# A state-space scan with a routed feed-forward part: one softplus, two row Silus, one block of drives and the last output products change places

## The reference, cut to what matters

```python
xn = layernorm(x)                                     # 2 rows of 1024 tokens, 512 wide
proj = xn @ W_in.T; x, gate = halves of 1024
x = silu(causal conv of x with 4 taps)
ts, Bm, Cm = rms(parts of x @ W_x.T)                  # 32, 16, 16 wide
dt = softplus(ts @ W_dt.T + b_dt)
state = state * exp(dt * A) + (dt * x) * Bm           # scan over time, 1024 channels x 16 states
y = (sum over states of state * Cm + x * D) * silu(gate)
s = y @ W_out.T
g = silu(top-2-of-8 experts of xn)                    # each token: weighted sum of two expert rows
out = x_in + s * g
```

## Time and profile before

| | |
|---|---|
| median of three runs | 1031.8 us |
| profiled execution | 1033.03 us |
| its span, first to last instruction | 1031.2 us |
| mean granted TensorE clock | 0.917 |
| busy: DVE, POOL, PE, ACT | 977.1, 908.9, 841.1, 731.3 us |

### The profile page before, as it was taken

How to read it: one execution, slowest core, us unless ns; L and a number is a source line. 1 busy time by engine, 2 the same in 40 slices (tenths; PEclk the granted TensorE clock), 3 DMA queues, 4 the chain that set the end, 5 groups by cost and what they waited for, 6 DMA issues and landing times.

```text
span 1031.2 us, 10504 instructions
## 1 busy us (share of the span) xinstructions
PE 841.1 (82%) x2832; PEld 321.6 (31%) x2832; DVE 977.1 (95%) x1026; ACT 731.3 (71%) x1283; POOL 908.9 (88%) x321
## 2 busy tenths in 40 slices
PE   9953579899788998999647859999887989979477
PEld 6520123333333333333212213333332333323122
DVE  6989999999999989999989899999999999999986
ACT  3657677798787767888655566888778776777542
POOL 0546899999989989998798999899988999999996
PEclk9976679999989999999876889999999999999788
DMA  9875688666777756566733742956648565663735
GB/s 342 333 251 211 227 288 298 258 259 235 266 277 265 263 221 235 210 218 211 235 105 116 234 176 102 321 194 219 208 162 294 171 233 190 224 242 125 272 55 143
DMA packets 82059, 229.22 MB, mean 222 GB/s; under 512 B 8784, under 2 KB 10320, under 8 KB 75344
## 3 DMA queue, kind: packets, MB, share of 16 engines
q1 hardware_dynamic: 67792, 197.08, 53.4%
q0 software_dynamic: 6144, 16.78, 6.3%
q10 hardware_dynamic: 8064, 14.68, 3.8%
HBM read 116.05 MB, written 45.35 MB: 157 GB/s over the span
## 4 chain that ended last, share of the span: by engine, by line
DVE 30%; POOL 22%; PE 17%; issue 14%; ACT 14%; DMA 2%; ACTq 0%; SPq 0%; DVEq 0%; POOLq 0%
POOL drive L622 13%; DVE sc_ps L1221 10%; DVE drive L1221 6%; POOL drive L635 5%; DVE drive L1232 5%; ACT sc_ps L837 5%; PE x_ps L1554 3%; PE dt_ps L1482 3%; PE y_ps L1522 2%; DVE x_ps L1145 2%; PE f_ps L1507 2%; POOL moe L607 2%; ACT L979 1%; PE x_ps L1416 1%; DVE xy L1145 1%
## 5 line engine op out<-in xcount | busy, mean ns | idle before, releaser
L622 POOL TENSOR_TENSOR drive<-rep,b_all 128x2048 f32<-128x2048 f32 x127 | 580.2, 4607 | 21.6 <-DMA rep<-dtu 13.2
L837 ACT ACTIVATE sc_ps<-rep,a_neg 128x512 f32<-128x512 f32 x512 | 332.5, 682 | 96.8 <-DVE drive L1232 73.3
L635 POOL TENSOR_TENSOR drive<-drive,c_all 128x1024 f32<-128x1024 f32 x94 | 225.5, 2399 | 20.4 <-ACT state L816 14.8
L1522 PE MATMUL y_ps<-drive,stack 128*32 128x512 f32 x1024 | 151.5, 666 | 96.6 <-DVE drive L1232 56.5
L1221 DVE TENSOR_TENSOR_SCAN sc_ps<-sc_ps,state,drive 128x512 f32<-128x512 f32 x162 | 200.4, 1275 | 6.4 <-ACT sc_ps L837 2.7
L1232 DVE TENSOR_TENSOR drive<-sc_ps,c_all 128x1024 f32<-128x1024 f32 x161 | 196.0, 1218 | 2.9
L1221 DVE TENSOR_TENSOR_SCAN sc_ps<-sc_ps,drive 128x512 f32<-128x512 f32 x160 | 188.9, 1216 | 7.0 <-ACT sc_ps L837 4.2
L1507 PE MATMUL f_ps<-w_ring,xT_slot 128*128 128x512 f32 x368 | 169.3, 603 | 24.2 <-ACT xT_slot L847 24.2
L1482 PE MATMUL dt_ps<-xnT,w_g 128*128 128x512 f32 x232 | 117.6, 653 | 20.0 <-ACT dtu L804 16.8
L1221 DVE TENSOR_TENSOR_SCAN drive<-sc_ps,state,drive 128x512 f32<-128x512 f32 x94 | 116.3, 1270 | 2.7 <-ACT sc_ps L837 2.6
L1221 DVE TENSOR_TENSOR_SCAN drive<-sc_ps,drive 128x512 f32<-128x512 f32 x96 | 114.6, 1212 | 1.2 <-ACT sc_ps L837 0.6
(11 more groups left out here) (192 smaller groups left out, 1038.2 us busy)
## 6 DMA issues: line engine op xcount, KB each, us to landing
rep<-dtu SPq DMA_DIRECT2D x128, 512.0 KB
w_ring<-wring SPq DMA_DIRECT2D x46, 1024.0 KB, 4.9
x_slot<-slot_x SPq DMA_DIRECT2D x46, 256.0 KB, 4.5
slot_rows<-y_slot ACTq DMA_DIRECT2D x46, 256.0 KB
w_g<-wg_in SPq DMA_DIRECT2D x32, 256.0 KB
w_x<-wx_in SPq DMA_DIRECT2D x24, 256.0 KB
slot_x<-zeros SPq DMA_DIRECT2D x1, 5888.0 KB, 20.3
slot_x<-zeros SPq DMA_DIRECT2D x5, 1024.0 KB, 8.7
```

Of the source, the lines that this page charges most:

```text
L622: pool.tensor_tensor(drive[:, m % RING, :, :], rep[:, n % 2, :, 1, :], b_all[:, q:q + 1, :].broadcast_to([P, NR, TC]), ALU.mult).then_inc( ...
L635: pool.tensor_tensor(drive[:, m % RING, 0:2, :], drive[:, m % RING, 0:2, :], c_all[:, q:q + 1, :].broadcast_to([P, 2, TC]), ALU.mult).then ...
L837: act.activation(sc[:, r, :], rep[:, n % 2, r, 0, :], ACT.Exp, scale=a_neg[:, lo:lo + 1]).then_inc(decay_ok, 1)
L1522: last = pe.matmul(y_ps[CH * r:CH * (r + 1), :], stack[:, :], drive[:, m % RING, r, :], start=False, stop=(m % NQ == NQ - 1))
```

## The change

- In tile 15, DVE's `step_sizes(16)` stands behind the high product of quad 0 instead of ahead of it.
- In tile 16, POOL issues `drives` of quad 3 ahead of `gather_first(1)`, and `drives` of tile 17's quad 0 ahead of `add_second(1)`; before, each stood behind. In tile 30 the order stays.
- In tiles 17 and 31, ACT's `silu_moe` stands between the skip diagonal and the decays of quad 1, between two table loads of its own. Before it shared the block of the gate's Silu. In tile 31 the gate's block moves ahead of the first half decays of quad 2 (`SILU_SOON`). Tile 15 keeps its rows' Silu where it was.
- In tile 31, PE does five of the nine output products that stood behind the sums of quad 1 ahead of them (the four others stay behind); output tile 3 does five instead of six products ahead of the last sums and one behind them, and its last two come after the last products of tiles 0 to 2.

```diff
-SILU_SOON = (24, 25, 26, 27, 28, 29, 30)
+SILU_SOON = (24, 25, 26, 27, 28, 29, 30, 31)
+STEPS_BEHIND = (15,)
+ROWS_FIRST = (17, 31)
...
                 low_products(NQ * n)
-                if gathers:
+                if gathers and not even:
                     gather_first(c - 1)
                 put_rows(*PUTS.get((n, 0), (0, 0)))
                 drives(NQ * n + 3)
                 low_products(NQ * n + 1)
-                if gathers:
+                if gathers and even:
+                    gather_first(c - 1)
+                elif gathers:
                     add_second(c - 1)
...
                 drives(NQ * n + 4)
+                if gathers and even:
+                    add_second(c - 1)
...
                 store_slot(b, left_slot)
+                if n in ROWS_FIRST:
+                    act.preload_act_table_set(SILU)
+                    silu_moe(c - 1, 0, TT)
+                    act.preload_act_table_set(LNEXP)
                 decays(m + 1, 0)
...
                     silu_gate(n)
-                    if (c and even and t == 1) or (not even and t == NT - 1):
+                    if n == PER_ROW * NT - 1:
                         silu_moe(c - 1, 0, TT)
...
-                    if chunk_end and not pe_log(n + 1):
+                    if chunk_end and not pe_log(n + 1) and n not in STEPS_BEHIND:
                         step_sizes(n + 1)
                     if n not in GATE_BEHIND:
                         gate_tile(n - 1)
                     products(m, 1)
+                    if n in STEPS_BEHIND:
+                        step_sizes(n + 1)
...
                 sums(m)
+                if c == NCH - 1 and t == NT - 1:
+                    out_tile(c, 0, t - 1, t)
+                    out_tile(c, 2, t - 1, t)
+                    out_tile(c, 1, 0, 3)
...
                 if c == NCH - 1 and t == NT - 1:
-                    out_tile(c, 0, t - 1, t)
-                    out_tile(c, 2, t - 1, t)
-                    out_tile(c, 1, 0, t)
+                    out_tile(c, 1, 3, t)
                 sums(m + 2)
...
-            out_tile(NCH - 1, 3, 0, NT - 2)
+            out_tile(NCH - 1, 3, 0, 5)
             sums(QUADS - 1)
-            out_tile(NCH - 1, 3, NT - 2, NT - 1)
-            for i in range(TT):
+            out_tile(NCH - 1, 3, 5, 6)
+            for i in range(TT - 1):
                 out_tile(NCH - 1, i, NT - 1, NT)
+            out_tile(NCH - 1, 3, 6, NT)
```

## The result

The changed kernel takes 1034.58 us (median of 20 runs, 1032.96 to 1036.43) against 1032.28 us of the kernel before in 20 runs. The ratio is 1.002, 95% interval 1.0013 to 1.0026: slower by 2.3 us, where 1031.6 and no measurable change were forecast and the range ended at 1034.0. The profiled execution took 1035.1 us with a span of 1033.3 us, 2.1 us longer than the one before.

What follows compares the result with a forecast made beforehand. DVE was taken to bound the kernel, busy 377.6 of 388 us from 612 to 1000 us. Tiles 15 to 17 at +3.0 us and the tail at -3.2 gave -0.2, so 1031.6 us, range 1028.0 to 1034.0.

Steps and rivals of the forecast that it cites:

- Steps 1 and 2: Tiles 15 and 16: softplus behind the high product, drives ahead of gathers; tile 17 begins 3.9 us sooner, last gather 4.6 later.
- step 1: Tile 15, DVE: the 1.21 us product fits into the wait for ACT's logarithm; what is queued behind starts 1.1 us sooner.
- Step 3: Tile 17, ACT: rows' Silu waits for the last gather; quad 1 starts 4.15 us after its landing, break-even landing at 594.3.
- Step 4: Tile 18's spread delays the last gather 3.3 us, to 597.3; tiles 15 to 17 cost +3.0 us (bounds -0.3, +4.9).
- rival B: Spread served first or in equal turns: all 5.2 us added to the gathers, landing 599.2, kernel 1033.5 us; chance 0.17.
- Rival A: Accumulating gathers not held up by the spread: landing 594.0, kernel 1028.3 us; chance 0.23.
- rival D: Another wait in tile 15 or 16 takes the 1.1 us; spread comes later, gather delay 2.6 us, kernel 1030.9; chance 0.12.
- Step 5: Tile 31, ACT: rows' Silu hidden with 1.0 us to spare; DVE's 1.14 us wait in quad 2 goes, gain 1.1.
- Step 6: Tail of tile 31: output products moved into PE's idle time; gain 3.2 us with the ACT edits' gain (bounds -3.4, -2.4).
- sign that the prediction named for being right: Tile 17: Silu about 597, DVE idle some 8 us, no quad 2 wait, step sizes near 586; tile 31: gate about 1 us behind.
- signs for being wrong: Tile 17's rows' Silu by 594 or after 599; tile 31: DVE waiting for quad 1 or 2 decays, or PE's products delaying sums.
- C: Tail of tile 31: TensorE's clock falls in shorter idle times, gain 2.4 instead of 3.2, kernel 1032.4 us; chance 0.08.

Runs made afterwards that it cites:

- Experiment 6: Kernel before with the tile 31 edits and the softplus of step_sizes(16) behind the high product, no other edits: 1030.81 us, ratio 0.9987.
- Experiments 1 and 2: Changed kernel with, first, tile 17's rows' Silu back in the gate's block: 1028.67 us, 0.9964; second, tile 16's gathers ahead of the drives again: 1029.51 us, 0.9974.
- Experiment 3: Changed kernel with SP holding tile 18's spread until tile 16's four accumulated gathers have landed: 1030.15 us, ratio 0.9976.
- experiment 4: Kernel before with the tile 31 edits on ACT and PE alone: 1030.96 us, ratio 0.9985.
- experiment 7: Kernel before with POOL's changed order in tile 16 and no other edit: 1030.66 us, ratio 0.9983.
- experiment 5: Tile 31 edits alone, with POOL's last three residual adds of chunk 2 cut to 8 of 512 columns: 1029.60 us against the kernel before, ratio 0.997.

## Why the prediction was wrong

**Steps 1 and 2 were right.** With the execution's lead of 1.3 us, tile 17 was forecast to begin at 586.0 - 1.3 = 584.7 and begins at 584.78; the last gather is issued at 586.96, forecast at 588.4 - 1.3 = 587.1. Experiment 6 shows that step 1 is worth nothing as long as POOL's drives set the pace of tile 16.

**Step 3 was right in mechanism and sum.** The Silu waits, quad 1 starts 600.83 - 596.61 = 4.22 us behind its start (4.15 forecast), and the whole stands and falls with the landing. Experiments 1 and 2 take away the early Silu and the late gathers, one at a time, and either frees the kernel. Experiment 3 takes away the spread beside the gathers and frees it in part.

**Step 4 had a term too small.** The delay is 4.1 us, not 3.3: 0.9 us for each of the 4.7 us of engine time left, where plain gathers had shown 0.7. That lies between the forecast and rival B, which put all 5.2 us on it. In the profile tiles 15 to 17 cost 3.6 us instead of 3.0. By the ratios of the changed kernel and experiment 4 they cost 0.35%, also 3.6 us, but with some 1.2 us of noise either way, so that the times alone wouldn't tell 3.6 from 3.0. Rival A, no delay, is refuted by the 9.5 us and by experiment 3. What rival D said of the size holds: experiment 7, where the spread comes 0.9 us later against the last gather, has 0.9 us less of delay.

**Step 5 was right.** In tile 31 the rows' Silu is hidden and DVE's wait of 1.14 us is gone.

**Step 6 is the one that failed.** "3.2" was right up to the gate product: 3.4 us of gain there against 3.3 forecast. It was worth 1.5 us in time (ratio 0.9985). I had looked at POOL's last residual adds only for the order of the stores ("its store is queued ahead of the last four") and taken DVE's chain behind the gate product as fixed in length (it is 7.1 us before, 9.3 in the changed kernel). But the gain brings DVE's first add, which reads both operands from SBUF, 3.4 us forward, while POOL's adds don't come sooner (they come 0.6 us later): into POOL's row of adds, which until then had ended 1.6 us ahead of it. It took 2.27 us more, shown with its cause by experiment 5. The Trainium skill, GPSIMD Engine Reference, section Key points, has the rule: GpSimd shares its SBUF interfaces with VectorE, and instructions of VectorE with two SBUF inputs contend. The rows agree: 2.95 us for the add from SBUF, 0.69 us for the products from PSUM beside the same adds.

With tiles 15 to 17 at the profile's 3.6 us and the tail at experiment 4's -1.5 the sum is +2.1 us; 2.3 were measured. Of the 2.3 us between this sum and the forecast of -0.2, 0.6 are step 4's and 1.7 step 6's. Step 6 alone lies outside its noise: experiment 4's interval ends at a gain of 2.6 us, and 3.2 were forecast.

Every sign that the prediction named for being right came true: the rows' Silu at 596.6, DVE idle 8.6 us ahead of quad 1, the gate product 1.27 us behind DVE's last product. None of the signs for being wrong did. They all concern waits, and the loss lay in the length of an instruction behind the last of them. The rivals on the slower side were the gathers (B) and PE's clock in the tail (C, 0.8 us); none put anything on the chain behind the gate product. So the range's upper end took the upper bound of the gathers with the whole gain of the tail.

## What to carry to other kernels

A result that arrives by DMA may be used sooner, or asked for later, but the two don't add: put the instruction that waits for it on an in-order engine no sooner than its last landing, and count in that landing what other transfers the same edit brings forward. An edit that makes one engine earlier at the end moves it against engines that stay; look for what it then runs beside, not only for what it waits for. And undo a bundle's parts one by one: here, with one edit of five taken back, the kernel is 5.8 us faster, and the four others together win 3.7.

## What the hardware showed that was not expected

- Accumulating gathers beside a spread of 2 MB and the start of the loads behind it: 8.6 to 9.5 us from issue to landing for the last of four, in four kernels, instead of 5.4 in experiment 3.
- A DVE add with both operands in SBUF was held back by a row of three POOL adds until about the end of the last one: 2.95 instead of 0.68 us, the same to 0.01 us in six kernels. POOL's adds stood back to back (4.27 us for three, as without DVE's). Only that add, the first, was held: the later ones came behind POOL's end.
- The same order of work on PE took 7.8 or 9.1 us for one output product of 16 matmul instructions, by where the granted clock came back: a difference of 1.3 us in DVE's wait behind it, between two kernels with the same instructions up to there.
